# A four-layer gated cross-attention kernel on one core: eight PSUM banks in one planned pool, weight copies in spaced pieces, setup in four parts, another order

## The chip, the core and the metric

The kernel runs on one core of a Trainium2 chip. It is one launch that takes all inputs from memory and leaves the output there. The metric is the time of that launch on the device in microseconds, the median of several runs. TensorE (PE) multiplies, VectorE (DVE) reduces and combines, ScalarE (ACT) copies out of PSUM and computes exp, tanh and gelu, GpSimd (POOL) does elementwise work on SBUF and issues the weight copies, SyncE (SP) issues nearly all other copies.

## The reference

Eight sequences of 256 rows of 128 features pass through four layers. Each layer is an attention over a context of 256 rows (16 heads of 8 features) and a feed-forward block (FFN), both gated by a tanh and added to x. In short:

```
for l in 0..3:
    x = x + tanh(g_xattn[l]) * attention_l(layernorm(x), ctx)
    x = x + tanh(g_ffn[l])   * ffn_l(layernorm(x))

attention_0, 1: softmax(q k' / sqrt(8)) v, heads joined, product with Wo, bias
attention_2:    the same with a causal mask
attention_3:    the same, only for the 51 of 256 rows of each head whose mean
                cosine with the keys is highest; the other rows give 0
ffn_0: the 192 rows with the highest router score pass gelu(x W), the others stay
ffn_1: 8 experts (128 -> 256 -> 128, silu(a) * b), the best two of a row weighted
       by a softmax, and a shared expert of double width
ffn_2: 8 experts (128 -> 512 -> 128, gelu), the best two weighted, and a shared one
ffn_3: x and weight rounded to a 6-bit grid in blocks of 32, product, bias
```

## The kernel before

**The work and its steps.** A sequence is called b (0 to 7). Four are in flight at a time, each with its own set of buffers s = b % 4 (SLOTS); sequence 4 takes over the buffers of sequence 0, and so on. `stream_steps` writes down one sequence as a list of small steps such as ("maxima", l, part). `TURNS_TAKEN` is a string of digits: each digit says whose next step comes next. `schedule()` makes SCHEDULE of it, 2280 steps. Every engine walks through this same list and issues its own part of each step, so the list is the order of work on every engine; the engines run apart as far as their semaphores let them.

**One attention.** "keys" and "query" make k and q by features (L787, L816); ScalarE copies them out, GpSimd splits each into three bf16 parts (L538 to L543), and SP moves the parts with six copies of 64 KB each into k_st and q_st (L496, L505). "maxima" (8 steps of a layer, 6 in the causal one) computes scores into two banks (L736), and VectorE takes the maximum of each row (L1248). "max_turn" turns these maxima (L853), ScalarE copies them to mT, and SP copies mT into rows of q_st, 16 KB (L509), so that the next product subtracts them. "attend" (8 steps) computes the scores again, turned (L755), into two banks, and ScalarE takes the exp (L643). TensorE waits for the copy of mT before part 0. "weigh" (8 steps) multiplies with the values (L775) into a bank C that is held for four steps, after which ScalarE copies it out (L650). "heads", "heads_turn" and "project" follow.

**The FFNs.** "norm" makes the layer norm's output h on GpSimd (L548, L552) from statistics by VectorE (L1200 to L1208), "turn" turns it (L715). Layer 1: "hidden" (L901) and "output" (L911). Layer 2: "hidden" (L932), gelu on ScalarE (L696), "output" (L941), and VectorE adds the weighted output to xs (L1129). Layer 3 is a chain of fourteen VectorE steps ("quantise", L982 to L1010) and one product.

**PSUM.** PSUM has eight banks of 512 fp32 columns. Three are a ring A, whose products VectorE reads (semaphores a_full and a_read), three a ring B, for ScalarE (b_full, b_read), two are C. `w.slot` gives product n of its kind the bank (n - 1) % 3, and `w.free` waits until product n - 3 has been read. `CREDIT` starts both counters at 3, so that the first products need not wait. A C bank goes to whichever sequence starts four weigh steps while one is free (`bank_holders`).

**Weights.** GpSimd issues `ffn_loads` (6 copies: the layer 0 block, router 1, all of layer 1) at the first weigh steps of sequence 0 in layer 0, two at each step, and `big_loads` (13 copies, eight of them 512 KB: layer 2) in the same way at the weigh steps of sequence 0 in layer 1 (L555 to L557). TensorE waits for all of ffn_loads at "route0" of layer 0 (L883), and for all of big_loads at "logits" of layer 2 (L892). ScalarE issues `late_loads` (the value weights and biases of layers 1 to 3, 580 KB) at the key step of sequence 3 (L623).

**The start.** VectorE clears the buffers of slots 0 and 1 (L955 to L958), GpSimd those of 2 and 3 (L439 to L442). VectorE then splits the first weights by heads (L963, semaphore first_ready), for which TensorE's first product waits. "keys" of sequence 0 is the first step of the list. After its "query" comes "setup": VectorE prepares some twenty small operands in one piece (L1138 to L1158), the memset of C (L1157) and of junk (L1158) among them.

## Time and profile before

| | us |
|---|---|
| median of 3 runs | 1022.35 |
| the runs | 1022.14, 1022.35, 1025.9 |
| the profiled execution, whole | 1025.37 |
| its span, first to last instruction | 1023.6 |

| engine | busy us | share of the span |
|---|---|---|
| TensorE, matmul | 914.3 | 89% |
| TensorE, weight load (beside matmul) | 606.6 | 59% |
| VectorE | 744.4 | 73% |
| ScalarE | 648.6 | 63% |
| GpSimd | 450.7 | 44% |

The mean granted clock of TensorE is 0.955 of 2.4 GHz. The profile is one execution. "Busy" counts the time in which an instruction of the engine is under way; matmuls overlap each other, and their ends are modelled. "Idle before" is the idle time of an engine just ahead of an instruction, and "<-" names what ended it; "issue" is said where the profile shows no releaser. In the table of stretches, the clock is a share of full speed and DMA the mean busy share of the 16 DMA engines. Steps are counted from the order in the code, times are read from the trace.

### The profile page before, as it was taken

How to read it: one execution, taken by the hardware profiler on the slowest of the kernel's cores; microseconds unless marked ns; L12 is line 12 of the kernel's file. 1: busy time of each engine (PE TensorE's matmuls, PEld its weight loads, DVE VectorE, ACT ScalarE, POOL GpSimd, SP SyncE). 2: the span in 40 equal slices, each digit the busy share in tenths (PEclk: the TensorE clock that was granted, in tenths of full speed). 3: DMA queues.
4: the chain of work that ended last, by engine and by line, in shares of the span. 5: the costliest groups of instructions: out<-in, count | busy, mean ns of one | idle time of the engine just before them, and what ended most of it. 6: DMA issues, size and time to landing. Idle time of an engine off the chain costs nothing.

```text
span 1023.6 us, 22491 instructions
## 1 busy us (share of the span) xinstructions
PE 914.3 (89%) x7921; PEld 606.6 (59%) x7921; DVE 744.4 (73%) x2544; ACT 648.6 (63%) x1445; POOL 450.7 (44%) x543
## 2 busy tenths in 40 slices
PE   3688759999999999999986898999999999999863
PEld 2234325775589888467643355646479987777422
DVE  5788859776645465898899999887854347756887
ACT  2377547776676536778674677776687547787640
POOL 6524543655366033355255265545551434342322
PEclk9699789999999999999998799999999999999976
DMA  6341261101011000002112111111010010000000
GB/s 158 94 109 50 73 176 34 29 24 47 3 46 29 9 16 18 19 24 55 26 29 59 30 45 44 32 34 33 19 49 2 17 32 18 3 23 11 19 3 21
DMA packets 67309, 39.92 MB, mean 39 GB/s; under 512 B 8055, under 2 KB 65168, under 8 KB 67200
## 3 DMA queue, kind: packets, MB, share of 16 engines
q1 hardware_dynamic: 63088, 29.85, 11.5%
q0 software_dynamic: 2016, 6.78, 2.3%
q10 hardware_dynamic: 2096, 1.85, 0.6%
q8 instruction: 66, 1.08, 0.4%
q14 instruction: 43, 0.35, 0.1%
HBM read 11.19 MB, written 1.05 MB: 12 GB/s over the span
## 4 chain that ended last, share of the span: by engine, by line
PE 72%; DVE 13%; ACT 5%; POOL 4%; issue 3%; DMA 1%; SPq 0%; ACTq 0%; DVEq 0%; POOLq 0%
PE A L941 12%; PE B L932 12%; PE C L775 9%; PE A L901 6%; PE B L755 6%; PE A L736 6%; DVE mx L1248 6%; PE A L722 4%; PE B L911 3%; ACT probs L643 3%; POOL h L552 3%; PE B L715 2%; PE A L872 2%; PE B L816 2%; PE B L762 2%
## 5 line engine op out<-in xcount | busy, mean ns | idle before, releaser
L1248 DVE TENSOR_REDUCE mx<-A 128x2 f32<-128x512 f32 (+1 forms) x480 | 306.6, 683 | 57.5 <-PE A L736 41.3
L643 ACT ACTIVATE probs<-B 128x512 f32<-128x512 f32 (+1 forms) x512 | 264.5, 569 | 97.3 <-PE B L755 69.4
L696 ACT ACTIVATE probs<-B,b_sb 128x256 f32<-128x256 f32 x288 | 118.7, 472 | 76.3 <-PE B L932 74.8
L775 PE MATMUL C<-probs,v_aug 128*9 128x256 f32 (+1 forms) x2048 | 152.4, 380 | 1.8 <-ACT probs L643 1.6
L548 POOL TENSOR_TENSOR rstd<-veps,mhalf 128x2 f32<-128x2 f32 x64 | 48.2, 753 | 236.1 <-DVE veps L1208 235.7
L941 PE MATMUL A<-w_sb,probs 128*128 128x128 f32 x1152 | 142.2, 277 | 0.1
L941 PEld LDWEIGHTS A<-w_sb,probs 128*128 128x128 f32 x1152 | 136.0, 192 | 7.0 <-issue 3.1
L932 PE MATMUL B<-hT,w_sb 128*128 128x256 f32 x576 | 139.2, 385 | 0.1
L736 PE MATMUL A<-k_st,q_st 64*128 64x256 bf16 (+1 forms) x1024 | 100.9, 281 | 30.5 <-DVE mx L1248 25.9
L755 PE MATMUL B<-q_st,k_st 64*128 64x256 bf16 (+1 forms) x1024 | 100.9, 275 | 26.7 <-issue 12.5
L582 POOL TENSOR_TENSOR rn<-ss,mhalf 128x32 f32<-128x32 f32 x16 | 88.0, 5503 | 75.4 <-DVE ss L1053 75.3
L932 PEld LDWEIGHTS B<-hT,w_sb 128*128 128x128 f32 x576 | 103.9, 190 | 17.6 <-issue 3.0
L1129 DVE SCALAR_TENSOR_TENSOR xs<-A,comb,xs 128x128 f32<-128x128 f32 x144 | 43.8, 345 | 86.7 <-PE A L941 82.5
L577 POOL TENSOR_TENSOR xs<-xs,raw 128x256 f32<-128x256 f32 x72 | 53.0, 736 | 115.8 <-ACT raw L684 92.3
L552 POOL TENSOR_SCALAR h<-xs,mv,rstd 128x128 f32<-128x128 f32 x112 | 91.0, 818 | 5.8
L736 PEld LDWEIGHTS A<-k_st,q_st 64*128 64x128 bf16 x1024 | 34.8, 95 | 95.3 <-DVE mx L1248 63.1
L755 PEld LDWEIGHTS B<-q_st,k_st 64*128 64x128 bf16 x1024 | 35.4, 95 | 94.2 <-ACT probs L643 48.1
L603 ACT ACTIVATE hT<-B 128x256 f32<-128x256 f32 x96 | 37.2, 387 | 75.9 <-PE B L715 75.4
L901 PE MATMUL A<-hT,fc_sb 128*128 128x256 f32 x320 | 77.0, 383 | 0.8 <-DVE probs L1369 0.7
L775 PEld LDWEIGHTS C<-probs,v_aug 128*9 128x9 f32 x2048 | 33.8, 89 | 58.6 <-issue 25.6
L538 POOL TENSOR_TENSOR resid<-resid,q_parts 128x256 f32<-128x256 f32 x32 | 23.1, 723 | 99.2 <-ACT resid L618 99.2
L901 PEld LDWEIGHTS A<-hT,fc_sb 128*128 128x128 f32 x320 | 57.5, 190 | 9.2 <-DVE probs L1369 1.7
(195 smaller groups left out, 1450.7 us busy)
## 6 DMA issues: line engine op xcount, KB each, us to landing
k_st<-k_parts SPq DMA_DIRECT2D x192, 64.0 KB, 2.0
q_st<-q_parts SPq DMA_DIRECT2D x192, 64.0 KB, 2.0
w_sb<-in_w POOLq DMA_DIRECT2D x8, 512.0 KB, 8.7
cT<-in_ctxT SPq DMA_DIRECT2D x8, 128.0 KB, 2.8
x_in<-in_x SPq DMA_DIRECT2D x8, 128.0 KB, 5.7
fc_sb<-in_fc POOLq DMA_DIRECT2D x1, 1024.0 KB, 6.8
out_x<-xs SPq DMA_DIRECT2D x8, 128.0 KB, 1.8
q_st<-mT SPq DMA_DIRECT2D x32, 16.0 KB
```

The lines of the kernel that those rows point to most:

```text
L552: ins = nc.gpsimd.tensor_scalar(h[s][:, r, :], (x_in if l == 0 else xs)[s][:, r, :], mv[s][:, r, 0:1], rstd[s][:, r:r + 1], ALU.subtract, ...
L577: nc.gpsimd.tensor_tensor(xs[s][:, :, :].rearrange("p t d -> p (t d)"), xs[s][:, :, :].rearrange("p t d -> p (t d)"), raw[s][:, n % OUT_RI ...
L582: nc.gpsimd.tensor_tensor(rn[s][:, :], ss[s][:, :], mhalf[:, :], ALU.pow)\
L643: nc.scalar.activation(probs[s][:, part % UNIT_RING, 2 * a:2 * a + 2, 0:n], b_bank(w, a + 1)[:, 0:2 * n].rearrange("p (j q) -> p j q", j=2 ...
L696: ins = nc.scalar.activation(hid[s][:, part % UNIT_RING, c, :], b_bank(w, half + 1)[:, j * ROWS:(j + 1) * ROWS], ACT.Gelu, bias=b1_sb[:, p ...
L736: ins = nc.tensor.matmul(a_bank(w, a + 1)[:, i * keys:(i + 1) * keys], head_rows(q_st, s, a, hp0 + i, r * P, P), head_rows(k_st, s, a, hp0 ...
L755: ins = nc.tensor.matmul(b_bank(w, a + 1)[:, j * n:(j + 1) * n], head_rows(k_st, s, a, 2 * g + j, t * P, P), head_rows(q_st, s, a, 2 * g + ...
L775: ins = nc.tensor.matmul(C[VW * i:VW * i + VR, C_BANK[b, l, u // 4], g % 2, q0:ROWS], v_aug[s][:, t, 4 * g + i, :], probs[s][:, u % UNIT_R ...
L901: ins = nc.tensor.matmul(a_bank(w, k + 1)[:, a * ROWS:(a + 1) * ROWS], fc1_sb[:, 2 * part + k, a, :], hT[s][:, :], start=True, stop=True)
L932: ins = nc.tensor.matmul(b_bank(w, half + 1)[:, j * ROWS:(j + 1) * ROWS], w1_sb[:, part, 2 * half + j, :], hT[s][:, :], start=True, stop=True)
L941: ins = nc.tensor.matmul(a_bank(w, 1)[:, r * D:(r + 1) * D], hid[s][:, part % UNIT_RING, c, r * P:(r + 1) * P], w2_sb[:, part, c, :], star ...
L1248: nc.vector.tensor_reduce(mx[s][:, r, a, hp0:hp0 + n], a_bank(w, a + 1).rearrange("p (n k) -> p n k", n=n), AX.X, ALU.max).then_inc(sems[" ...
```

## The change

- **Banks.** A, B and C become one array `banks` of eight. A second string of 1857 digits, `BANKS_TAKEN`, names the bank of each product in the order of the list: 1793 products of the kinds a and b and 64 holdings of four weigh steps. `bank_holders` notes for each which read came last on the same bank, and `wait_bank` waits for that read, be it a_read, b_read or c_read. CREDIT goes. A bank that nobody has had before isn't waited for.
- **Order.** `TURNS_TAKEN` is new throughout, 2304 digits. 24 more steps come from the setup in four parts (8 sequences of 3 more); only those of sequence 0 issue anything. The keys of layer 0 now stand behind the statistics and the norm in a sequence's list. Aside from setup, half of the steps stand at most two places from where they stood, and 1694 of 2272 at most five. The list now begins with the statistics and norm of sequence 0 and statistics of 2 and 1, then keys 0.
- **Weights.** No copy is over 256 KB. The layer 0 block has its own list and semaphore (1 copy at step 90); `ffn_loads` are 9 copies, one every 9 steps from step 110 to 182, and the wait for them moves from route0 to the logits of layer 1; `big_loads` are 21 copies, one every 12 steps from step 230 to 470. The steps at which they are needed first are route0 at 125, logits of layer 1 at 313 and of layer 2 at 586. `late_loads` are issued at step 50, which is the first attend of sequence 0.
- **Start.** VectorE clears slot 0 alone, GpSimd 1 to 3. VectorE zeroes all eight banks (128x512 each) ahead of the split of the first weights. The memset of C goes. Setup is four steps, and all who wait for it wait for the fourth.

```diff
-RING = 3
+BANKS = 8
 CBANKS = 2
-DVE_SLOTS = 2
+DVE_SLOTS = 1
 EARLY_LOADS = 3
+BLK_AT, FFN_AT, FFN_EVERY, BIG_AT, BIG_EVERY, LATE_AT = 90, 110, 9, 230, 12, 50
...
-ROW_PARTS, KEY_ROW_PARTS, FP6_PARTS = 5, 3, 14
+ROW_PARTS, KEY_ROW_PARTS, FP6_PARTS, SETUP_PARTS = 5, 3, 14, 4
...
-    out = [("keys", 0, 0)]
+    out = []
     for l in range(LAYERS):
-        out += norm(l) + [("turn", l, 0), ("query", l, 0)] + [("setup", 0, 0)] * (l == 0)
+        out += norm(l) + [("keys", 0, 0)] * (l == 0) + [("turn", l, 0), ("query", l, 0)]
+        out += [("setup", 0, part) for part in range(SETUP_PARTS)] * (l == 0)
...
-0000111001021122333000300000200210310121331010010100211002100120120020021021102101121032120120130120
...
+0002112031300110212030300001100210000001102313311101021020020130001121221000200201200211301321131120
...
+BANKS_TAKEN = """
+1023546720315462703154626703154267031524670315246371045620347562034170536472056347025613024763102746
...
+107602753416025735416027354160735416207351620734516207345
+"""
...
+    def take(kind, n, read):
+        bank[kind, n] = int(next(digits))
+        before[kind, n] = last.get(bank[kind, n])
+        last[bank[kind, n]] = read
...
+    for i, (step, b, l, part) in enumerate(SCHEDULE):
+        for kind in "ab":
+            for k in range(signals(step, b, l, part).get(f"{kind}_full", 0)):
+                n = LEDGER.index(i, f"{kind}_full", k + 1)
+                take(kind, n, (f"{kind}_read", n))
+        if step == "weigh" and part % 4 == 0:
+            end = STEP["weigh", b, l, part + 3]
+            take("c", (b, l, part // 4), ("c_read", LEDGER.index(end, "c_read", 1)))
+    return bank, before
...
+    def last_read(self, kind, k):
+
+        return READ_BEFORE[kind, LEDGER.index(self.i, f"{kind}_full", k)]
...
-        A = psum("A", [P, RING, BANK])
-        B = psum("B", [P, RING, BANK])
-        C = psum("C", [P, CBANKS, 2, ROWS])
+        banks = psum("banks", [P, BANKS, BANK])
...
+        blk_loads = [(blk0[:, :], block0)]
+        ffn_loads = [(r1_sb[:, :], router1)]
+        for e in range(0, EXPERTS, 2):
+            ffn_loads.append((fc1_sb[:, e:e + 2, :, :].rearrange("d e a i -> d e (a i)"), fc1.rearrange("e d i -> d e i")[:, e:e + 2, :]))
+        for e in range(0, EXPERTS, 4):
+            ffn_loads.append((fc2_sb[:, e:e + 4, :], fc2.rearrange("e i d -> i e d")[:, e:e + 4, :]))
+        ffn_loads += [
             (fc1_sb[:, EXPERTS:EXPERTS + 2, :, :], gate_up),
-            (fc2_sb[:, 0:EXPERTS, :], fc2.rearrange("e i d -> i e d")),
             (fc2_sb[:, EXPERTS:EXPERTS + 2, :], down.rearrange("(c i) d -> i c d", c=2))]
...
+        big_loads = [(r2_sb[:, :], router2), (b1_sb[:, :, :], b1_cols), (b2_sb[:, :], b2_all)]
+        for e in range(EXPERTS):
+            big_loads += [
+                (w1_sb[:, e, :, :].rearrange("d c i -> d (c i)"), w1[e, :, :]),
+                (w2_sb[:, e, :, :], w2[e, :, :].rearrange("(c i) d -> i c d", c=HC))]
+        big_loads += [
             (w1_sb[:, EXPERTS, :, :].rearrange("d c i -> d (c i)"), ws1),
             (w2_sb[:, EXPERTS, :, :], ws2.rearrange("(c i) d -> i c d", c=HC))]
...
-                if step == "weigh" and b == 0 and l < 2:
-                    for dst, src in (ffn_loads if l == 0 else big_loads)[part * 2:part * 2 + 2]:
-                        pool.dma_start(dst, src).then_inc(ffn_loaded if l == 0 else big_loaded, 16)
+                for first, every, loads, loaded in ((BLK_AT, 1, blk_loads, blk_loaded), (FFN_AT, FFN_EVERY, ffn_loads, ffn_loaded), (BIG_AT, BIG_EVERY, big_loads, big_loaded)):
+                    if w.i >= first and (w.i - first) % every == 0 and (w.i - first) // every < len(loads):
+                        pool.dma_start(*loads[(w.i - first) // every]).then_inc(loaded, 16)
...
-                if step == "keys" and (b, l) == (SLOTS - 1, 0):
+                if w.i == LATE_AT:
                     for dst, src in late_loads:
                         act.dma_start(dst, src).then_inc(late_loaded, 16)
...
+            def wait_bank(kind, k):
+
+                if w.last_read(kind, k):
+                    name, value = w.last_read(kind, k)
+                    pe.wait_ge(sems[name], value)
+
             def turn_rows(k, src):
 
-                pe.wait_ge(sems["b_read"], w.free("b_read", k))
+                wait_bank("b", k)
...
-                    pe.wait_ge(sems["a_read"], w.free("a_read", a + 1))
+                    wait_bank("a", a + 1)
...
-                if u % 4 == 0 and C_BEFORE[b, l, u // 4] is not None:
-
-                    pe.wait_ge(sems["c_read"], w.at_step("c_read", 1, *C_BEFORE[b, l, u // 4]))
+                if u % 4 == 0 and READ_BEFORE["c", (b, l, u // 4)]:
+                    name, value = READ_BEFORE["c", (b, l, u // 4)]
+                    pe.wait_ge(sems[name], value)
...
-                    pe.wait_ge(sems["a_read"], w.free("a_read", 1))
+                    wait_bank("a", 1)
                     rows_product(a_bank(w, 1), coT[s], wvo[:, l, 1, :]).then_inc(sems["a_full"], 1)
                 if step == "route0" and part == 0:
-                    pe.wait_ge(ffn_loaded, 16 * len(ffn_loads))
+                    pe.wait_ge(blk_loaded, 16 * len(blk_loads))
                     pe.wait_ge(sems["b_read"], w.at_step("b_read", 1, "turn", b, LAYERS, 0))
-                    pe.wait_ge(sems["a_read"], w.free("a_read", 1))
+                    wait_bank("a", 1)
                     nc.tensor.matmul(a_bank(w, 1)[:, 0:ROWS], r0_bc[:, :], hT[s][:, :], start=True, stop=True)\
                         .then_inc(sems["a_full"], 1)
...
-            dve.sem_inc(sems["a_read"], CREDIT["a_read"])
             nc.vector.memset(mhalf[:, :], -0.5)
             for s in range(DVE_SLOTS):
                 clear(nc.vector, s, cleared_dve)
+            for n in range(BANKS):
+                nc.vector.memset(banks[:, n, :], 0.0)
...
+            def set_up(part):
+
+                if part == 0:
+                    dve.wait_ge(attn_loaded, 16 * len(attention_loads))
+                    dve.wait_ge(gates_done, 1)
...
+                if part == 1:
...
+                if part == 2:
+                    for n in range(1, LAYERS):
...
+                if part == 3:
...
+                    nc.vector.memset(mean_k[:, :], 1.0 / ROWS)
+                    ins = nc.vector.memset(junk[:, :, :], 0.0)
+                ins.then_inc(setup_done, 1)
```

## Rows read from the trace of the kernel before

**Rows 1.** Page, parts 1 and 5: engine, busy us, share, instructions; costliest group.
```profile
PE 914.3 (89%) x7921; PEld 606.6 (59%) x7921; DVE 744.4 (73%) x2544; ACT 648.6 (63%) x1445; POOL 450.7 (44%) x543
...
L1248 DVE TENSOR_REDUCE mx<-A 128x2 f32<-128x512 f32 (+1 forms) x480 | 306.6, 683 | 57.5 <-PE A L736 41.3
```

**Rows 2.** Stretches: length, busy us of PE PEld DVE ACT POOL, clock, DMA, GB/s.
```profile
28.00:46.00 18.00, 10.55 (x64) 3.93 (x62) 15.62 (x32) 2.91 (x8) 9.40 (x16) 0.59 0.34 91
...
300.00:400.00 100.00, 100.00 (x710) 87.01 (x709) 52.96 (x180) 51.82 (x121) 31.68 (x32) 1.00 0.08 21
...
500.00:600.00 100.00, 81.26 (x822) 37.85 (x820) 93.67 (x309) 63.89 (x131) 42.89 (x54) 0.91 0.13 32
...
950.00:1000.00 50.00, 38.27 (x376) 17.01 (x376) 41.94 (x191) 27.03 (x54) 16.91 (x17) 0.86 0.04 11
```

**Rows 3.** Stretches again: the three holes, and the stretch behind each.
```profile
57.90:61.10 3.20, 0.01 (x2) 0.04 (x3) 1.30 (x3) 0.17 (x1) 0.00 (x0) 1.00 0.84 222
...
61.10:66.00 4.90, 4.90 (x44) 2.26 (x44) 2.74 (x5) 3.59 (x7) 0.00 (x0) 0.65 0.02 3
...
118.70:120.70 2.00, 0.06 (x1) 0.01 (x1) 1.34 (x8) 0.00 (x0) 0.54 (x1) 0.50 0.15 59
...
120.70:130.00 9.30, 8.79 (x70) 3.47 (x70) 5.85 (x14) 6.54 (x13) 4.05 (x6) 0.67 0.00 0
...
140.80:150.40 9.60, 0.03 (x2) 0.06 (x4) 0.63 (x2) 0.00 (x0) 0.00 (x0) 0.66 0.93 282
...
150.40:158.00 7.60, 7.52 (x64) 3.44 (x64) 5.12 (x21) 5.52 (x11) 3.36 (x5) 0.76 0.04 9
```

**Rows 4.** Timeline, 133 to 151 us: start, length, engine, what, [idle before].
```profile
133.86 4.91 POOL L557 DMA_DIRECT2D w_sb<-in_w  x6
...
139.85 0.59 SPq L509 DMA_DIRECT2D q_st<-mT  x1
...
150.37 0.61 PE L755 MATMUL B<-q_st,k_st 64*128 64x256 bf16 x4 [10.16 <-issue]
```

**Rows 5.** Waits of TensorE, whole span: us in total, times, longest.
```profile
PE A L736 <- DVE mx L1248: 25.9, 36, 2.3
...
PE B L755 <- ACT probs L643: 6.2, 21, 0.8
...
PE B L755 <- DMA q_st<-mT: 3.2, 1, 3.2
```

**Rows 6.** DMA issues: whole span, then 135-152, 100-150, 0-30 us; KB, landing.
```profile
k_st<-k_parts SPq DMA_DIRECT2D x192, 64.0 KB, 2.0
...
k_st<-k_parts SPq DMA_DIRECT2D x6, 64.0 KB, 9.5
...
w_sb<-in_ws POOLq DMA_DIRECT2D x2, 256.0 KB, 3.8
...
x_in<-in_x SPq DMA_DIRECT2D x4, 128.0 KB, 6.6
```

**Rows 7.** Timeline and chain of the start: start us, length, what.
```profile
1.15 0.91 DVE L439 MEMSET q_st<- 128x1024 f32 x1 [0.16 <-issue]
...
2.91 0.59 SPq L454 DMA_DIRECT2D x_in<-in_x  x1
...
4.53 5.31 DMA bv_all<-in_bias_rows
...
5.46 0.36 DVE L963 COPY wqk<-probs 128x128 f32<-128x128 f32 x2
...
11.64 0.48 DVE L1200 BATCH_NORM_STATS2 stats<-x_in 128x6 f32<-128x128 f32 x2
...
20.40 0.91 DVE L1157 MEMSET C<- 128x1024 f32 x1 [0.21 <-issue]
...
21.41 0.48 DVE L1158 MEMSET junk<- 128x512 f32 x1
...
28.05 0.39 PE L736 MATMUL A<-k_st,q_st 64*128 64x256 bf16 x4
```

More of the change, by code:

```diff
@@ L148 @@
+4777
 """
@@ L203, in signals @@
     }[step]
-CREDIT = {"a_read": RING, "b_read": RING}
-def bank_holders():
-    free, bank, before = [(None, n) for n in range(CBANKS)], {}, {}
-    for step, b, l, part in SCHEDULE:
-        if step == "weigh" and part % 4 == 0:
-            assert free, "more than two streams hold a bank of the weighed values"
-            before[b, l, part // 4], bank[b, l, part // 4] = free.pop(0)
-        if step == "weigh" and part % 4 == 3:
-            free.append(((step, b, l, part), bank[b, l, part // 4]))
-    return bank, before
@@ L246, with bank_holders @@
 STEP = {item: i for i, item in enumerate(SCHEDULE)}
+def bank_holders():
+    digits = iter("".join(BANKS_TAKEN.split()))
+    bank, before, last, weighed, holding = {}, {}, {}, {}, {}
+    def take(kind, n, read):
[11 more added lines that the diff above has]
+    return bank, before
+BANK_OF, READ_BEFORE = bank_holders()
 class Walk:
```

194 lines of the change are left out of this document (97 added, 97 removed).

## Prediction

> **What bounds the kernel now.** I read the page's first part, then the table of stretches, the waits of TensorE, and two stretches of the timeline. TensorE is busy for 914.3 of 1023.6 us, VectorE for 744.4 [rows 1]. So the kernel runs at TensorE's pace wherever TensorE has work, and what can be won quickly is its idle time of 109 us and what its wait for others and a low clock stretch. The table says where that is. In the middle there is nothing idle: from 300 to 400 us TensorE is busy for 100.00 of 100 us at full clock [rows 2]. Time gained ahead of such a stretch is passed on to the end, because nothing else waits there. The idle time is in other places:
>
> - Three holes in which nearly every engine stands still: 57.9 to 61.1, 118.7 to 120.7 and 140.8 to 150.4 us, with TensorE busy for 0.01, 0.06 and 0.03 us of them. In the last one VectorE works 0.63 us and ScalarE and GpSimd not at all, while the DMA engines are 0.93 busy and move 282 GB/s [rows 3].
> - Stretches in which VectorE paces: 28 to 46 us (VectorE 15.62 of 18.00), 500 to 600 (93.67 of 100) and 950 to 1000 (41.94 of 50) [rows 2].
> - The start: TensorE's first score product stands at 28.05 us [rows 7].
>
> **Part 1: spaced weight pieces.** What is the last hole? GpSimd issues six copies of expert weights, 512 KB each, one behind the other from 133.86 to 138.77 us. At 139.85 SP issues the 16 KB copy of the turned maxima into q_st, and the next score product that needs it (L755) starts at 150.37 [rows 4]. The profile puts that wait down to "issue", which names nobody; the hole at 57.9 has the same shape and there the releaser is named, the DMA q_st<-mT, 3.2 us [rows 5]. In the same burst the 64 KB copies of the key parts took 9.5 us to land, where the median of all 192 is 2.0 us [rows 6]. So a small transfer that the attention waits for sits behind megabytes of weights that nobody needs yet. The hole at 118.7 follows the first three large copies of layer 2 in the same way.
>
> The change issues 31 weight copies in place of 19, none over 256 KB: the FFN pieces every 9 steps from step 110, those of layer 2 every 12 steps from step 230. 2280 steps in 1023.6 us are 0.45 us a step, so a 256 KB piece comes each 5.4 us (about 49 GB/s asked for), and a copy of that size landed in 3.8 us [rows 6]: each is done before the next is issued. The dates hold: counted in the two orders, the last FFN piece is issued at step 182 and first needed at 313, the last of layer 2 at 470 and needed at 586, over 50 us ahead in both cases. The wait in route0 is now for its own 64 KB block alone.
>
> What goes: the three holes, 3.19 + 1.94 + 9.57 = 14.7 us of TensorE idle [rows 3]. TensorE comes out of each with a lower granted clock: 0.65 over 4.9 us, 0.67 over 9.3 us and 0.76 over 7.6 us [rows 3]. A mean of g between the two levels means that (1-g) of the stretch is what half speed costs a TensorE that is bound: 1.7 + 3.1 + 1.8 = 6.6 us. Part of each stretch is paced by exps and maxima, so I take half, 3.3 us (bounds 0 and 6.6). When the stall goes, what is late next is the reduce of the maxima, at the pace of the stretch around it.
>
> What it costs: the six issues took 4.91 us of GpSimd, 0.82 us each [rows 4]. 12 more of them are at most 9.8 us of an engine that is busy 44% [rows 1]; they stand ahead of the h of a norm, the split of q and k and the x plus bias in GpSimd's order, and SP's copies behind a split move with them; only where TensorE waits for one of these does it show. I take +1 us, bounds 0 and 9.8. The pieces still meet the small copies, but one at a time; that is within the same bound.
>
> A rule speaks against this part. The Trainium skill, "DMA: Bandwidth & Descriptors", section "Queues, rings and completion order", says that each DMA engine goes round the queues that have work and switches after a packet. By it a 16 KB copy on SP's queue would pass a burst on GpSimd's queue after a few packets, and would not be ten us late. No row here separates packets; the 9.5 us against 2.0 us above speak against it in this kernel, and by the rule the holes would stay (a rival, below).
>
> **Part 2: one pool of eight banks.** Before, products for VectorE turn through three banks A, those for ScalarE through three B, and two C hold weighed values. Every new product waits for the third last of its kind. I counted, in the two orders, how many steps lie between the step that reads a bank and the step that takes it again: of 1849 takes 268 are three steps or less before, 42 after; the least is one step before and two after. The C kind loses reserve (mean 47 steps before, 8.5 after; least 4). What such waits cost today: TensorE idle for maxima behind the reduce (L736 on L1248) 25.9 us, for scores behind the exps 6.2 us [rows 5], together 32.1 us. But a bank doesn't make VectorE faster. In the stretches where it paces, no more can be won than its own idle time: 2.4 + 6.3 + 8.1 = 16.8 us [rows 2]. The other end is no gain. I take 9 us, just over the middle, since the near reuses fall to a sixth; the "order searched anew" is in this figure. The new order is a neighbour of the old: half of the steps moved by two places or less, on average by four, and the mix of steps in each twenty-fourth of the list is nearly unchanged, so I give it no gain of its own.
>
> **Part 3: the start.** Before, TensorE's first A product waits for bv_all (issued at 4.53 us, 5.31 us until it lands), VectorE stands behind it, and the first row statistics start at 11.64 us [rows 7]. Now they stand first. They need x of batch 0, which is issued at 2.91 us [rows 7]; the four copies of x took 6.6 us in the median [rows 6], which puts it at 9.5 us at the latest. VectorE is ready at 7.3: it now clears one slot in place of two (two memsets of 0.91 and small ones less, 2.0 us) and zeroes eight banks (8 x 0.48, the row of junk, of the same width), 1.9 us more than before, so it splits the first weights at 7.3 in place of 5.46 [rows 7]. That is covered by the load of bv_all, which lands at 9.84; without that cover it would cost 1.9 us. So the first statistics stand at 7.3 to 9.5 us in place of 11.64, and the chain through h, q and the first maxima starts 2.1 to 4.3 us sooner. The setup in four parts lets other work in between and loses the memset of C (0.91 us) [rows 7]; ScalarE's late loads move from the key step of batch 3 to step 50, where it waits for the first maxima to land anyway. Some of the gain meets the pace of the maxima: I take 3 us (bounds 0 and 6).
>
> Each product's wait stays one wait on one semaphore, and 24 more steps in the list issue nothing: 0 us.
>
> **Sum.** -14.7 - 3.3 + 1 - 9 - 3 = -29.0 us. The profiled execution took 1025.37 us, of which 1023.6 span; it lies at the upper end of the three runs (median 1022.35), so the same change of the span gives 996 for the profiled one and 993 for the median.
>
> **The rivals.**
> *The holes go, but VectorE keeps the pace and takes the rest.* Banks and start bring nothing, since VectorE is busy 94% in its stretches [rows 2], and the pieces' meetings with small copies cost some 5 us: -14.7 - 3.3 + 5 = -13, 1009 us. For it: the reduce lasts as long as before. Against: the chain of the start is latency, not VectorE's work.
> *The holes are not the burst's.* If a hole belongs to the order or to something the profile doesn't show, it stays: -9 - 3 + 1 gives 1011 us. By the rule on queues of the Trainium skill's page "DMA: Bandwidth & Descriptors" this is the case that comes. Against it are the 9.5 us landings [rows 6] and three holes at three bursts.
> *The pool and order bring all they can.* -14.7 - 6.6 - 16.8 - 6 = -44, 978 us.
> *Slower: products for ScalarE now wait for VectorE.* In the new plan 392 takes of a bank for ScalarE have VectorE as the last reader, none before. VectorE runs late in its stretches; then scores that only ScalarE needs stand behind a reduce of 0.68 us (mean of 480 [rows 1]), and TensorE works in order, so all behind it wait as well. It eats the gain of 29 us once 43 of the 392 come a reduce late; if one in four does, 98 x 0.68 = 67 us, 1060 us. Against it: only 21 of the 392 are reused within four steps.
>
> **How the numbers follow.** The forecast (985 to 1003) has 0.47, the full gain (down to 970) 0.17, VectorE's pace 0.14, holes that stay 0.08, a result within 0.5% from a mixture of these 0.06, slower 0.08. The likeliest is 993. From the best case, 978, less 4 for what the order may add, to the 1009 and 1011 of the two weak cases: 974 to 1012. Half a per cent, 5 us, is about what a measurement of this kernel can tell from no change: faster 0.86, within 0.06, slower 0.08.
>
> **What the profile after would show.** Part 1: no stretch of over 2 us in the first 300 us in which all engines stand still; DMA's rate under some 150 GB/s from 60 to 260 us; the small copies landing in 2 to 4 us at all times. Part 2: TensorE's waits on L1248 and on the exps down from 32 us to some 20, VectorE over 95% busy around 500 to 600. Part 3: the first score product near 24 us. It would be wrong if a wait of scores on a VectorE reader turned up among the longest, if TensorE waited for a weight piece (fc_sb, w_sb), or if a hole stood where no weights move.

## The result, and the profile after

The changed kernel takes 978.91 us (median of 4 runs, 974.97 to 983.77) beside 1024.12 us for the kernel before on the same chip: a ratio of 0.956, 95% interval 0.950 to 0.961. I had forecast 993 us, in a range of 974 to 1012. The sign and the range held; the gain is 45 us where the sum said 29. Of the experiments below, e5, e6, e8 and e9 ran on another chip, on which the kernel before took 1026.50 us; beside runs of the first chip, their ratios to before are the safer measure. The profiled execution took 980.12 us, 978.3 of them span.

The page of after, parts 1 and 5 (columns as in [rows 1]):

```profile
PE 893.3 (91%) x7921; PEld 611.1 (62%) x7921; DVE 738.0 (75%) x2547; ACT 633.8 (65%) x1443; POOL 459.0 (47%) x559
...
L1295 DVE TENSOR_REDUCE mx<-banks 128x2 f32<-128x512 f32 (+1 forms) x480 | 299.1, 680 | 30.4 <-PE banks L776 24.8
```

TensorE executes the same 7921 products, but its idle time went from 109.3 to 85.0 us and its busy time from 914.3 to 893.3 [rows 1]. The prediction had spoken of idle time and of the clock behind the holes, and of nothing else. VectorE's reduces cost what they did; its idle time ahead of them fell from 57.5 to 30.4 us, of which the waits for the products they read are 41.3 [rows 1] and 24.8.

Stretches of after (columns as in [rows 2]); the first one covers the time in which the second and the third hole stood before:

```profile
60.00:260.00 200.00, 186.95 (x1824) 112.99 (x1821) 161.39 (x531) 141.01 (x348) 115.36 (x163) 0.98 0.26 68
300.00:400.00 100.00, 99.49 (x830) 80.40 (x830) 60.72 (x196) 56.92 (x131) 27.16 (x26) 1.00 0.07 17
500.00:600.00 100.00, 82.61 (x756) 44.92 (x753) 92.22 (x322) 62.94 (x145) 48.40 (x67) 0.90 0.17 44
```

The waits of TensorE in after (us in total, times, longest):

```profile
PE banks L755 <- POOL h L587: 14.5, 17, 2.5
PE banks L755 <- DVE h L1053: 11.9, 3, 11.5
PE banks L893 <- DVE m_parts L1308: 9.8, 7, 3.7
...
PE banks L776 <- DVE mx L1295: 4.9, 6, 2.5
...
PE banks L795 <- DVE mx L1295: 3.9, 4, 2.3
...
PE banks L795 <- DMA q_st<-mT: 2.4, 1, 2.4
```

L776 is the old L736, L795 the old L755. The 25.9 us behind the reduce [rows 5] are 4.9, or 8.8 with the scores for ScalarE (L795), which now can wait for VectorE too. The waits of the scores for ScalarE put down to "issue" were 12.5 us in before, 10.2 of them the last hole; now they are 0.6. From 40 to 400 us TensorE waits for more than 2 us only once, 2.31 us at 127 us, and that is one of the scores for ScalarE behind a reduce. What stands on top now is the chain of a new block: h from GpSimd, and the split maxima (m_parts). The 11.5 us behind h from VectorE stand at 969 us, in the last layer of the last sequence. No wait for a weight piece shows. The small copies landed in at most 4.9 us (k_st) and 4.8 us (q_st), near the 2 to 4 that I had expected; the DMA rate reached 207 GB/s in a slice of 5 us between 60 and 260 us, more than my "some 150".

The start of after (timeline: start, length, what):

```profile
7.41 0.30 DVE L1006 COPY wqk<-probs 128x128 f32<-128x128 f32 x2
7.62 0.49 DVE L1247 BATCH_NORM_STATS2 stats<-x_in 128x6 f32<-128x128 f32 x2
...
22.62 0.98 PE L776 MATMUL banks<-k_st,q_st 64*128 64x256 bf16 x12
```

The first statistics stand at 7.62 us in place of 11.64, the first score product at 22.62 in place of 28.05 [rows 7].

### The profile page after: what moved, and what is told of

It is laid out like the page before. It is cut to its first block, busy times and chain, and to the rows that moved or that the text cites. A ratio compares the mean times of both kernels' runs of the same rounds, so it can differ in the third digit from the quotient of the medians.

```text
span 978.3 us, 22501 instructions
## 1 busy us (share of the span) xinstructions
PE 893.3 (91%) x7921; PEld 611.1 (62%) x7921; DVE 738.0 (75%) x2547; ACT 633.8 (65%) x1443; POOL 459.0 (47%) x559
## 4 chain that ended last, share of the span: by engine, by line
PE 69%; DVE 17%; POOL 5%; ACT 4%; issue 3%; DMA 1%; SPq 1%; ACTq 0%; DVEq 0%; POOLq 0%
PE banks L983 12%; PE banks L974 12%; PE banks L815 9%; DVE mx L1295 6%; PE banks L795 6%; PE banks L943 5%; PE banks L776 5%; PE banks L762 4%; POOL h L587 3%; PE banks L953 3%; PE banks L912 3%; PE banks L755 2%; ACT probs L677 2%; PE banks L802 2%; PE banks L856 2%
## 5 line engine op out<-in xcount | busy, mean ns | idle before, releaser
L1295 DVE TENSOR_REDUCE mx<-banks 128x2 f32<-128x512 f32 (+1 forms) x480 | 299.1, 680 | 30.4 <-PE banks L776 24.8
L677 ACT ACTIVATE probs<-banks 128x512 f32<-128x512 f32 (+1 forms) x512 | 259.5, 578 | 66.4 <-PE banks L795 42.3
L730 ACT ACTIVATE probs<-banks,b_sb 128x256 f32<-128x256 f32 x288 | 118.6, 471 | 86.5 <-PE banks L974 84.7
L815 PE MATMUL banks<-probs,v_aug 128*9 128x256 f32 (+1 forms) x2048 | 149.8, 377 | 5.0 <-ACT probs L677 4.0
L983 PE MATMUL banks<-w_sb,probs 128*128 128x128 f32 x1152 | 140.9, 276 | 0.0
L617 POOL TENSOR_TENSOR rn<-ss,mhalf 128x32 f32<-128x32 f32 x16 | 87.9, 5496 | 109.4 <-DVE ss L1096 109.3
L983 PEld LDWEIGHTS banks<-w_sb,probs 128*128 128x128 f32 x1152 | 136.1, 192 | 4.9 <-issue 2.5
L974 PE MATMUL banks<-hT,w_sb 128*128 128x256 f32 x576 | 137.2, 382 | 0.0
L974 PEld LDWEIGHTS banks<-hT,w_sb 128*128 128x128 f32 x576 | 104.4, 190 | 14.3 <-issue 1.5
L795 PE MATMUL banks<-q_st,k_st 64*128 64x256 bf16 (+1 forms) x1024 | 98.5, 275 | 7.9 <-DVE mx L1295 3.9
L776 PE MATMUL banks<-k_st,q_st 64*128 64x256 bf16 (+1 forms) x1024 | 91.6, 276 | 8.3 <-DVE mx L1295 4.9
L795 PEld LDWEIGHTS banks<-q_st,k_st 64*128 64x128 bf16 x1024 | 33.9, 95 | 79.9 <-issue 32.0
L776 PEld LDWEIGHTS banks<-k_st,q_st 64*128 64x128 bf16 x1024 | 38.5, 96 | 51.7 <-issue 17.3
```

What stands on the lines that cost most here:

```text
L617: nc.gpsimd.tensor_tensor(rn[s][:, :], ss[s][:, :], mhalf[:, :], ALU.pow)\
L677: nc.scalar.activation(probs[s][:, part % UNIT_RING, 2 * a:2 * a + 2, 0:n], b_bank(w, a + 1)[:, 0:2 * n].rearrange("p (j q) -> p j q", j=2 ...
L730: ins = nc.scalar.activation(hid[s][:, part % UNIT_RING, c, :], b_bank(w, half + 1)[:, j * ROWS:(j + 1) * ROWS], ACT.Gelu, bias=b1_sb[:, p ...
L776: ins = nc.tensor.matmul(a_bank(w, a + 1)[:, i * keys:(i + 1) * keys], head_rows(q_st, s, a, hp0 + i, r * P, P), head_rows(k_st, s, a, hp0 ...
L795: ins = nc.tensor.matmul(b_bank(w, a + 1)[:, j * n:(j + 1) * n], head_rows(k_st, s, a, 2 * g + j, t * P, P), head_rows(q_st, s, a, 2 * g + ...
L815: ins = nc.tensor.matmul(c_bank(b, l, u // 4)[VW * i:VW * i + VR, g % 2, q0:ROWS], v_aug[s][:, t, 4 * g + i, :], probs[s][:, u % UNIT_RING ...
```

## Where the time went: six marks

To place the gain I follow six marks through the traces: the start of ScalarE's copy mT of a sequence's turned maxima, or of GpSimd's rstd of a sequence's norm. The first column is the time of the mark before, the others are differences from it in us. The middle columns belong to experiments, told below: e1 has the old kernel with the new weight pieces, e5 adds the pool with a simple bank plan, e10 has a bank plan by measured times in its place, e11 adds the new order and start.

| mark | before | e1 | e5 | e10 | e11 | after | e12 |
|---|---|---|---|---|---|---|---|
| first maxima, sequence 0 | 41.7 | -0.8 | -0.8 | -0.9 | -5.6 | -5.3 | -7.5 |
| norm of sequence 0 ahead of FFN layer 1 (behind the last hole) | 154.4 | -16.3 | -20.3 | -18.7 | -22.9 | -24.6 | -29.2 |
| norm of sequence 0, attention layer 3 | 344.1 | -10.8 | -17.1 | -16.1 | -23.8 | -25.5 | -30.4 |
| maxima of sequence 5, layer 0 | 518.4 | -10.8 | -15.0 | -18.6 | -32.9 | -34.7 | -39.9 |
| norm of sequence 7, layer 2 | 801.8 | -10.6 | -14.2 | -21.0 | -38.1 | -38.7 | -45.1 |
| norm of sequence 7, last FFN | 1004.9 | -10.3 | -16.7 | -25.8 | -45.4 | -45.4 | -52.5 |

In after, 24.6 us are won by the end of the last hole, and 20.8 more on the 850 us behind it. The prediction had 17 + 3 for the first stretch, and nearly all of the pool's 9 for the rest. Each column is one execution.

## The experiments

**e1: the weight pieces alone.** The kernel before with the new lists of weight copies, issued by step number (at the places that correspond in the old order) in place of two in every weigh step:

```
-                if step == "weigh" and b == 0 and l < 2:
-                    for dst, src in (ffn_loads if l == 0 else big_loads)[part * 2:part * 2 + 2]:
+                for first, every, loads, loaded in ((BLK_AT, 1, blk_loads, blk_loaded), (FFN_AT, FFN_EVERY, ffn_loads, ffn_loaded), (BIG_AT, BIG_EVERY, big_loads, big_loaded)):
+                    if w.i >= first and (w.i - first) % every == 0 and (w.i - first) // every < len(loads):
```

> The kernel before with one part of the change, the spaced weight pieces and their waits: block at step 79, FFN pieces every 9 steps from 103, those of layer 2 every 12 from 216, the same items in the old order as in the changed kernel. Order, rings and start as before. Theory 'the bursts make the holes': all three holes go, 15 to 18 us, 1024 -> 1006 to 1009 (ratio 0.982 to 0.985), and no copy of k or q parts lands later than 5 us behind step 79. Rival 'the holes belong to the order': within 3 us of before, a hole stays near 140 us.

Measured: 1013.51 us, ratio 0.989 (0.985 to 0.992) to 1025.47: 12 us, less than the 15 to 18 of the theory, and far from the rival's "within 3 us". The stretches of e1 at the places of the three holes (before: 0.01, 0.06 and 0.03 us of TensorE [rows 3]), and two of its waits:

```profile
57.90:61.10 3.20, 3.11 (x40) 1.59 (x37) 3.20 (x8) 2.94 (x6) 0.00 (x0) 1.00 0.12 35
118.70:120.70 2.00, 1.95 (x24) 0.66 (x22) 1.97 (x8) 1.68 (x5) 1.27 (x3) 1.00 0.00 0
140.80:150.40 9.60, 9.49 (x96) 4.41 (x94) 8.06 (x14) 7.49 (x17) 6.96 (x12) 1.00 0.37 91
```
```profile
PE B L718 <- POOL h L555: 13.7, 13, 4.8
...
PE B L758 <- issue: 4.8, 4, 2.3
```

All three holes are full of work and the clock stands at 1.00 in them. At the mark behind the last one 16.3 us are won, as the sum had it (17); by 202 us it is 10.4, and from there it stays, 10.8 and 10.6 us at marks 450 us apart. So time won ahead of the busy middle does reach the end, and part of the hole's gain is given back at once. Most of what is given back can be seen. In e1 the work between the last hole and the mark at 202 us lies at 137.8 to 191.9 us; TensorE is idle there for 3.6 us, where before it was for 0.7 (154.0 to 202.3 us). The largest piece of it is a wait of 2.3 us at 154 us, behind three pieces that GpSimd issued from 149.55 to 152.14. And the granted clock, 1.00 in that stretch of before, is 0.94 over 12.2 us and 0.89 over 15.0 us in e1, which is 2.4 us for a bound TensorE. Over the whole span TensorE's idle time fell by 9.7 us (109.3 to 99.6), not by 14.7, and the mean clock is 0.955 in both:

```profile
PE 913.4 (90%) x7921; PEld 606.6 (60%) x7921; DVE 746.0 (74%) x2544; ACT 648.0 (64%) x1445; POOL 457.1 (45%) x555
```

No copy of k or q parts behind the start took 5 us to land, as expected.

**e4: the bursts alone, back in the changed kernel.** The inverse: the large copies in the first weigh steps again, all else as changed.

```
+                if step == "weigh" and b == 0 and l < 2:
...
+                    each = 2
+                    for dst, src in loads[part * each:part * each + each]:
```

> The changed kernel with the weight copies as before: 512 KB copies, two at a time at the weigh steps of sequence 0 in layers 0 and 1. Theory 'the bursts make the holes': 13 to 20 us slower than the changed kernel, 992 to 999, with holes of up to 10 us behind the bursts in which the score products wait for the 16 KB copy of the maxima. Rival 'the holes belong to the old order': within 4 us of 979.

Measured: 986.91 us, 0.962 (0.960 to 0.964), 8 us above the changed kernel (6 by the ratios). That is about half of the 13 to 20 that I expected, and more than the rival's 4. Two waits carry it, the first and the last hole again (timeline), each behind a burst:

```profile
PE banks L798 <- issue: 12.9, 2, 9.5
```
```profile
55.84 0.61 PE L798 MATMUL banks<-q_st,k_st 64*128 64x256 bf16 x4 [3.47 <-issue]
...
137.33 0.61 PE L798 MATMUL banks<-q_st,k_st 64*128 64x256 bf16 x4 [9.48 <-issue]
```

The short hole in the middle, which the profile of before puts down to VectorE (xs, 1.96 us), doesn't come back; for that one only e1 speaks. As in e1, the holes cost less than they are long: 12.9 us of waiting, 10.9 us against after at the mark behind them, 7.4 us at the last mark.

**e7: small pieces in bursts.** The changed kernel with its own small pieces, but two or three issued in each of the first weigh steps: in layer 1 of sequence 0 up to three of 256 KB a step, where before had up to two of 512 KB.

```
+                if step == "weigh" and b == 0 and l < 2:
...
+                    each = (2 if l == 0 else 3)
+                    for dst, src in loads[part * each:part * each + each]:
```

> The changed kernel with its small weight pieces (128 to 256 KB), but all issued in bursts, two or three in each of the first weigh steps of the first two layers. Theory A (what counts is how much is queued at once): as with the old copies, 985 to 990 us, ratio 0.960 to 0.965. Theory B (what counts is the size of one copy, small ones letting others in between): as the changed kernel, 977 to 981, ratio 0.953 to 0.956.

Measured: 985.69 us, 0.962 (0.960 to 0.965): as slow as the large copies in a burst, as theory A had it. Smaller copies alone don't remove the cost; spreading them does. The longest such wait is shorter, though, 5.18 us in place of 9.48, and each step queues fewer bytes, so size and amount aren't wholly separated here (timeline):

```profile
134.31 0.61 PE L799 MATMUL banks<-q_st,k_st 64*128 64x256 bf16 x4 [5.18 <-issue]
```

**e9: the pieces from SyncE.** The changed kernel with the three lines that issue pieces moved from GpSimd's list to SyncE's.

```
-                        pool.dma_start(*loads[(w.i - first) // every]).then_inc(loaded, 16)
+                        sp.dma_start(*loads[(w.i - first) // every]).then_inc(loaded, 16)
```

> The changed kernel with the 31 weight copies issued by SyncE at the same steps in place of GpSimd. GpSimd runs ahead through steps in which it has nothing to do, so its pieces come in groups (118.8, 120.1, 120.7 and 121.5 us); SyncE waits in nearly each attention, and issues them apart. Theory 'what is left of the weights' price is the grouping': the 2.4 us wait of the scores for the copy of the maxima goes, 2 to 5 us less, 974 to 977. Rival 'the pieces cost nothing any more': within 1.5 us of 979. Against both: a 256 KB copy ahead of the parts of q and k in SyncE's own queue delays them, 982 to 988.

Measured: 977.70 us, 0.953 (0.950 to 0.956). Within what the measurement can tell of the changed kernel; its marks lie 1.0 to 2.4 us earlier from 105 us on. The rival "the pieces cost nothing any more" held. The theory was wrong about the wait of 2.4 us: it stands at 940 us in after, where no weights move, and is still there in e9. What e9 does change is told with e8.

**e2 and e5: the pool without the new order.** Order and start as before; the eight banks in one pool. Each product takes the bank whose last reader comes first in the list of steps. e2 keeps the bursts, e5 has the spaced pieces.

```
+                bank = min(until, key=lambda m: (until[m], m))
+                until[bank] = reads[kind, n]
```

> The old order and the old bursts of weights, with the pool of eight banks. The bank of each product is chosen as the one whose last reading step is earliest in the list, since the planned string fits only the new order; start as before but for eight memsets of banks in place of the one of C (3.3 us more of VectorE ahead of the first weights). Theory 'the pool frees TensorE': 10 to 18 us less than before in spite of the start, 1006 to 1014, TensorE's waits for the reduces of the maxima fall from 26 us to under 10. Rival 'the order brings it, the pool alone little': 1022 to 1027 (the memsets lengthen the start), the waits only change their name.

> The old order and old start with both the pool (bank of the earliest last reading step, eight memsets at the start) and the spaced weight pieces; what is left to the changed kernel is its order and its start. Theory 'weights and pool add up': 0.9885 x 0.9932 = 0.982, 1006 us, so that 27 us of the changed kernel's gain are order and start. Rival 'with the holes gone the pool brings more, as theory of the pool had it': 995 to 1000.

Measured: e2 1017.72 us, 0.993 (0.991 to 0.996), a gain of 8. That lies between its two cases; the waits behind the reduces of the maxima fell to 12.0 us, not under 10. e5 1009.36 us, 0.983 (0.979 to 0.987), only 4 to 5 us under e1, with intervals that overlap. So with the holes gone the pool brings no more than it does beside them, and the rival of e5 (995 to 1000) falls.

**e3: the new order without the pool.** The changed kernel with three rings (3 + 3 + 2 banks) in its bank string.

```
+                bank = (n - 1) % 3 + (3 if kind == "b" else 0)
```

> The changed kernel with rings again: banks 0 to 2 in turn for VectorE's products, 3 to 5 for ScalarE's, 6 and 7 for weighed values. Order, start and weight pieces as changed. Theory 'the pool frees TensorE': 12 to 20 us slower than the changed kernel, 991 to 999 against 979. Rival 'the order brings it': within 5 us of the changed kernel, 979 to 984.

Measured: 1119.58 us, 1.093 (1.086 to 1.100), 141 us above the changed kernel. I had expected 12 to 20; neither theory came near. Two waits of TensorE carry it (L802 and L821 are the two score lines):

```profile
PE banks L802 <- DVE mx L1321: 75.8, 90, 3.6
PE banks L821 <- ACT probs L703: 34.7, 60, 2.4
```

The loss against before grows steadily, 9 us at the mark of 344 and 94 at the last. Counted as in the prediction, the new order with rings has 354 reuses within three steps, 64 of them within one; the old order had 268 and 19. The new order leans on the pool.

**e6: the planned string replaced by the simple plan.** Order, start and pieces of the changed kernel; the bank rule of e2.

> The changed kernel with the bank of each product chosen by the plain rule (the one whose last reading step is earliest in the list) in place of the planned string; 208 of 1857 banks are the same. Theory 'a pool of eight is what the new order needs, whatever the plan': within 5 us of 979. Rival 'the plan is part of the gain': 5 to 15 us slower, with scores waiting for readers of the other engine.

Measured: 1001.44 us, 0.975 (0.971 to 0.979), 22 us above the changed kernel (20 by the ratios), more than the rival's 5 to 15. The waits for maxima are back (L802, L821 as in e3):

```profile
PE banks L802 <- DVE mx L1321: 13.3, 22, 2.5
...
PE banks L821 <- DVE mx L1321: 6.2, 10, 1.9
```

So what does the string know? The trace gives the end of each reading instruction, and I looked up at each of the 1857 takes how many free banks had been read earlier than the one taken. The planned string takes the earliest at 1640 places, counted in the trace of after; the simple plan at 1261, counted in its own, where 85 takes had a bank free over 1 us earlier (planned: 16). Steps of the list are no measure of time: counted in steps the simple plan even looks better, with 2 reuses within three steps where the planned string has 42.

**e10 and e11: a bank plan by measured times.** Each product takes the bank whose last reader ended first in a trace: e10 is e5 with a string from e5's trace (old order), e11 the changed kernel with the trace of after. The kernel holds the resulting digits; of e11 the first line:

```
-1023546720315462703154626703154267031524670315246371045620347562034170536472056347025613024763102746
...
+0123456712305467120354671620354716203574162035741602354176035471603256407351647035614720613572061537
```

> The order, the start and the weight pieces of the run with pool and pieces in the old order (ratio 0.983 to before); only the bank string is new: each output takes the bank whose last reader had finished first in the trace of that run, where the simple plan took the bank of the earliest reading step. Theory A (what a pool is worth lies in planning it by the time at which the readers are done, in either order): the 22 us that the simple plan cost the changed kernel come back here too, 985 to 992 us, ratio 0.960 to 0.968, and the waits for VectorE's maxima fall under 10 us. Theory B (the planned string pays only together with the new order, which was searched with it): no more than 4 us come back, 1005 to 1010 us, ratio 0.979 to 0.985.

> The changed kernel with its bank string replaced by one made from the trace of the changed kernel: at each output the bank whose last reader ended first there. It agrees with the planned string in 247 of 1857 digits, but that one too takes the bank read earliest in 1640 of 1857 places, and the simple plan in 1235. Theory A (time of the last reading is all that the string is about): 976 to 981 us, ratio 0.951 to 0.957. Theory B (the string holds something more, such as keeping banks for later outputs): 985 to 1001 us, between the planned string and the simple plan.

Measured: e11 979.13 us, 0.954 (0.951 to 0.956). It is as fast as the planned string: a plan made from the times of the last readings alone does all that the string does (theory A). The 247 equal digits make the two look more different than they are, since the number of a bank is only a name. Counted by which earlier product had the bank, the two plans agree at 1431 of 1857 takes, the simple plan and the planned string at 700. e10: 999.38 us, 0.974 (0.972 to 0.977), 10 us under e5. That is between the two theories: the plan by time pays in the old order, by about half, and 20 us are left between e10 and e11 that belong to order and start. The waits of e10, whose L774 and L793 are the score lines:

```profile
PE banks L753 <- POOL h L585: 20.4, 19, 3.9
...
PE banks L825 <- DVE wqk L1004: 10.1, 1, 10.1
PE banks L774 <- DVE mx L1294: 7.1, 9, 1.3
...
PE banks L793 <- DVE mx L1294: 3.6, 4, 1.5
```

**e8: the setup in one piece.** The changed kernel with all four parts at the first of them.

```
-                    set_up(part)
+                    for n in range(SETUP_PARTS if part == 0 else 0):
+                        set_up(n)
```

> The changed kernel with the whole setup at its first part (step 15 of the list), in one piece as before. Theory 'the start's gain is that the statistics stand first': first maxima and all behind them within 1 us of the changed kernel, 978 to 981. Rival 'the split of setup brings it': VectorE holds the statistics of sequence 3 and the values up by 4 us, and the end comes 3 to 5 us later, 982 to 984.

Measured: 976.69 us, 0.951 (0.948 to 0.954): no slower. The split of the setup brings nothing. What is left for the start is that the statistics stand ahead of the keys; no run tests that by itself. Up to 90 us e8 is even 2.2 us ahead, and then loses it. The stretch 80 to 90 us, in after, e8 and e9 in this order:

```profile
80.00:90.00 10.00, 6.91 (x42) 4.18 (x42) 6.77 (x31) 5.51 (x14) 5.23 (x8) 0.83 0.53 147
```
```profile
80.00:90.00 10.00, 8.69 (x46) 5.12 (x46) 6.26 (x33) 5.34 (x13) 3.34 (x7) 0.57 0.39 110
```
```profile
80.00:90.00 10.00, 7.47 (x64) 4.33 (x67) 8.71 (x40) 6.62 (x16) 3.55 (x5) 1.00 0.54 150
```

TensorE's granted clock falls to 0.83 and 0.57 where GpSimd issues the pieces, and stays at 1.00 where SyncE does. In e11, where GpSimd issues them too, it is 0.66. The timeline of GpSimd in e8 shows what lies ahead: two issues take 1.58 us right before the x plus bias, the rstd and the h that TensorE waits 1.62 us for. In after the same wait is 1.63 us; in e9, which differs from after only in the engine that issues, it is 0.72 us.

```profile
74.54 1.58 POOL L592 DMA_DIRECT2D fc_sb<-in_fc  x2
76.13 0.74 POOL L601 TENSOR_TENSOR xs<-x_in,gbo 128x256 f32<-128x256 f32 x1
76.82 0.75 POOL L583 TENSOR_TENSOR rstd<-veps,mhalf 128x2 f32<-128x2 f32 x1
77.67 1.59 POOL L587 TENSOR_SCALAR h<-xs,mv,rstd 128x128 f32<-128x128 f32 x2
```

**e12: what the experiments point to.** The changed kernel with e8's setup, e9's issues, and a bank string from e8's trace.

> The changed kernel with the setup in one piece, the weight pieces issued by SyncE, and a bank string made from the trace of the changed kernel with the setup in one piece. Each part alone measured 2.2 and 1.2 us under the changed kernel or within its spread. If they add up: 972 to 976 us, ratio 0.947 to 0.951; if they were spread only: 976 to 980.

Measured: 973.16 us (971.45 to 976.80), 0.950 (0.948 to 0.952), beside 979.13 (975.68 to 979.53) for e11 on the same chip. It has the lowest time of all, as the case "they add up" had it, though the ranges of the single runs still touch. The gain over e11 stands in the first 120 us (6.3 us at 118) and stays. Against e8 it wins 4.5 us between two marks that stand at 72.5 and 115.4 us in before (0.2 us ahead there, then 4.7). Here h comes at 76.44, TensorE waits 0.69 us for it, and the clock keeps 1.00:

```profile
74.21 0.92 POOL L601 TENSOR_TENSOR xs<-x_in,gbo 128x256 f32<-128x256 f32 x1
...
76.44 1.58 POOL L590 TENSOR_SCALAR h<-xs,mv,rstd 128x128 f32<-128x128 f32 x2
```
```profile
80.00:90.00 10.00, 8.02 (x91) 4.02 (x88) 8.60 (x36) 7.10 (x16) 5.00 (x7) 1.00 0.41 111
```

## Why the prediction came out as it did

The measured decomposition, each step beside its term: weight pieces -12 (e1), predicted -14.7 - 3.3 + 1 = -17; pool with a plan by time in the old order -14 (e10 against e1), predicted -9; order and start together -20 (e11 against e10), predicted -3. Together 47 us for e11 (45 for the changed kernel), against 29. (The ratios give 12, 15 and 21.) So 978.91 lies 14 us from the forecast and inside its range, with two terms too small and one too large. That it is inside is in part luck: the lower end of the range came from the bounds of holes, clock, pool and start, and not from the order, which brought the most. It lies on the time of the rival in which pool and order bring all they can (978), but not by its terms: that one had 21.3 us for holes and clock where e1 gave 12, and nothing for the order itself.

**Part 1, the holes.** The mechanism was right: remove the bursts and the holes are gone, bring them back and two of them are back, 3.5 and 9.5 us. At the mark behind the last hole 16.3 us are won, of 18 for holes and clock. What failed is what comes behind it. The sum of part 1 had +1 us for the cost; 12 us measured leave some 6 us for it, inside the bounds of 0 to 9.8. The clock term of 3.3 us isn't seen either: the mean clock is 0.955 before and in e1, where it was low again behind the last hole's place. How the 6 us divide between the pieces' meetings with small copies and what is made up behind a hole in any case stays open; e4 has the second without spaced pieces (10.9 us at the mark behind its holes, 7.4 at the end). One cause is a statement that was wrong: "a 256 KB piece comes each 5.4 us", "each is done before the next is issued". The list's steps are no clock: GpSimd runs through steps that ask nothing of it, so pieces left in groups, in after at 118.8, 120.1, 120.7 and 121.5 us and then none until 135.5, in e1 three between 149.55 and 152.14, ahead of the wait of 2.3 us. The price of one issue held better: e11 and e12 differ on GpSimd by its 31 issues, and the page has 458.5 us busy (559 instructions) against 438.5 (528), 0.65 us each where I took 0.82. What it does beside is what I had left as "only where TensorE waits for one of these": at 77 to 80 us it did, and the low clock behind that wait can cost more than the wait. In e8 10 us at 0.57 are 4.3 us for a bound TensorE, and 4.5 us is what e8 loses to e12 there.

**The rival of the queues.** The three holes were gone with the bursts, so this case fell. But I had read the rule on queues too simply. These are the DMA views of before, 133.8 to 151 us, and 139 to 148 us, while both queues had work:

```profile
DMA packets 2126, 4.19 MB, mean 244 GB/s; under 512 B 247, under 2 KB 1226, under 8 KB 2126
...
q0 software_dynamic: 1008, 3.67, 71.0%
q1 hardware_dynamic: 1118, 0.52, 12.6%
```
```profile
q0 software_dynamic: 713, 2.60, 89.4%
q1 hardware_dynamic: 698, 0.32, 14.4%
```

The copies of SyncE's queue are not small in packets: 0.52 MB in 1118 packets (465 B each), beside 3.67 MB of weights in 1008 (3.6 KB each). The 16 KB copy of the maxima was issued behind six copies of key parts on its own queue. From 139 to 148 us the two queues moved nearly the same number of packets, 713 and 698, and in each single microsecond of it the counts lie within 6 of one another (88 and 88, 91 and 91, 87 and 86 in three of them). So packets of 465 B passed at the pace of packets of 3.6 KB, and the late landing of the copy of the maxima fits the six copies of 64 KB ahead of it on its own queue. The rule of the Trainium skill, "DMA: Bandwidth & Descriptors", section "Queues, rings and completion order", is that each DMA engine goes round the queues that have work, a packet at a time; the equal counts agree with it, if a packet of the profile is what the rule means. What I had left out is the queue ahead of the small copy. In e7 the pieces were smaller and a hole stayed. No run here changed the size of a packet or moved the small copy to a queue of its own.

**Part 2, the pool.** "A bank doesn't make VectorE faster" was right, and in size the bound for the pool held: 14 us against 16.8. It didn't hold by place. I had allowed a gain only in the stretches that VectorE paces; between the marks of e1 and e10 5.4 us are won up to 344 us, and of the whole 15.5 us up to the last mark only some 7 in the three stretches (28 to 46, 500 to 600, 950 to 1000). The value taken, 9, was low. What I missed is that the pool's worth is in its plan. With the simple plan it brought 8 us alone (e2) and 4 to 5 beside the spaced pieces (e5), and it cost the changed kernel some 20 (e6). I had compared reuses by steps, 268 against 42; the simple plan has 2 and is slower, so that count doesn't measure the worth of a plan. The forecast waits, 32 to some 20 us, fell to 10.7 (8.8 behind maxima, 1.9 behind the exps). "VectorE over 95% busy around 500 to 600" was wrong: 92.22 of 100, less than the 93.67 before. TensorE got what it needed without a busier VectorE.

**The order.** "A neighbour of the old; I give it no gain of its own" failed, and is the largest miss. What the search for it might bring was to be inside the pool's 9 us. With rings that order (with the new start and pieces) is 106 us slower than the old one with the same pieces (e3 against e1), with a timed pool 20 us faster (e11 against e10); 2.5 to 4.7 of the 20 are the start. Between e10 and e11 TensorE's idle time falls from 92.5 to 86.0 us, and its busy time from 904.6 to 891.4. The clock explains about 6 us of that at most: the share of the span below full clock, (1 - 0.954) x 997.1 = 45.9 us in e10, is (1 - 0.959) x 977.4 = 40.1 in e11. And the busy time of one group of products shrinks at a nearly unchanged mean. The score products for the maxima in the groups by line (busy us, mean ns, idle us before them and its releasers), of before and of after:

```profile
L736 PE MATMUL A<-k_st,q_st 64*128 64x256 bf16 (+1 forms) x1024 | 100.9, 281 | 30.5 <-DVE mx L1248 25.9 <-DVE resid L1278 3.0 <-DMA q_st<-q_parts 0.5
```
```profile
L776 PE MATMUL banks<-k_st,q_st 64*128 64x256 bf16 (+1 forms) x1024 | 91.6, 276 | 8.3 <-DVE mx L1295 4.9 <-ACT probs L677 1.2 <-DVE v_aug L1228 1.0
```

1024 products of 0.28 us are some 285 us end to end; they fill 100.9 us or 91.6 (97.4 in e10, 91.6 in e11: most of it comes with the order and start), because several are under way at once. So "busy" held time that another sequence gave back, and a busy engine is no floor. By the marks, 10 of the 20 us between e10 and e11 are won from 154 to 518 us. Which moves of the new order do it stays open.

**Part 3, the start.** Right in place and near in size: statistics at 7.62 us (forecast 7.3 to 9.5), the first score product at 22.62 (24), 4.7 us between e10 and e11 at the first mark and 2.5 at 91 us, for a term of 3 us. The four parts of the setup had no share in it (e8). That the statistics ahead of the keys make the rest is argued from the timeline.

**The slower rival.** Scores for ScalarE do wait for VectorE readers now, 4 times for 3.9 us in all; in e6, with the simple plan, 10 times for 6.2. It is real and small as long as the plan goes by time. The sign that I had named for it showed all the same: the longest wait of TensorE between 40 and 400 us is one of these, 2.31 us.

**Pace of VectorE as the rest.** It fell: the reduces took as long as before (680 ns against 683) and some 34 us came on top of e1.

## What to carry to other kernels

Plan shared buffers by the measured time at which each is released, taken from a trace of the kernel, not by a count of steps; in one and the same order that was worth 10 to some 20 us of 1000. Spread a background load over time, and check in the trace when the issuing engine comes to it; keep it off an engine whose next result TensorE waits for. An order and the buffers it was searched with belong together: judge neither alone, and don't take a busy engine's time for its least.

## What the runs showed of the hardware

- A queue of small transfers is held up by a burst on another: 64 KB copies with a median of 2.0 us took 9.5 [rows 6] beside 3.67 MB of weights, and cutting the same bytes into 256 KB copies left a wait of 5.18 us (e7). With work on both queues they moved equal numbers of packets: 713 of 3.6 KB and 698 of 0.46 KB in 9 us (before).
- A short wait can cost more than itself: behind one of 1.62 us TensorE's granted clock had a mean of 0.57 over 10 us, most of it at the lower of its two levels, 1.2 GHz (e8); behind one of 0.69 us (e12) and one of 0.72 us (e9) it stayed at the upper, 2.4 GHz. In after a wait of the same 1.63 us was followed by 0.83. These are single executions, and the engine's work around the waits differs too.
- A copy issued on GpSimd keeps it busy for 0.65 us (20.0 us for 31 issues, e11 against e12); on SyncE the same issues cost no time that the marks show (e9).
